# A Flamingo block with routed experts on one core: logits ordered from one comparison and its transpose, a first hand-out for a single tile, and a rearranged prelude and last batch

## What is computed

```python
# x (8, 256, 256), ctx (8, 77, 256); 16 heads of 16; 4 experts of width 1024, top 2
q, k, v = norm(x) @ wq + bq, ctx @ wk + bk, ctx @ wv + bv
score = (q @ k.T / 4) * mask;  score = where(score == 0, -1e9, score)
x = x + tanh(g0) * ((softmax(score) @ v) @ wo + bo)
t = norm(x).reshape(2048, 256)
logits = t @ router_w + router_b
top_p, top_i = top_k(softmax(logits), 2);  top_p /= top_p.sum(-1)
out = sum over chosen experts e of top_p * (silu(t @ w1[e]) * (t @ w3[e])) @ w2[e]
x = x + tanh(g1) * out
```

## Time and profile before

| what | value |
| --- | --- |
| median of 3 runs | 487.54 us (487.33 to 488.08) |
| the profiled execution | 488.64 us |
| its span in the trace | 486.7 us |
| mean granted clock of PE | 0.989 |
| PE busy | 460.7 us (95%) |
| DVE busy | 378.6 us (78%) |
| ACT busy | 307.0 us (63%) |
| POOL busy | 196.0 us (40%) |

### The profile page before, as it was taken

One profiled execution on the slowest core, in us unless ns is written; L12 is line 12 of the kernel. 1 busy time (PEld: TensorE's weight loads), 2 busy tenths in 40 slices (PEclk: granted clock), 3 DMA queues, 4 the chain that ended last, 5 costly groups with the idle time before them and its releaser, 6 DMA issues.

```text
span 486.7 us, 11552 instructions
## 1 busy us (share of the span) xinstructions
PE 460.7 (95%) x3720; PEld 433.4 (89%) x3720; DVE 378.6 (78%) x876; ACT 307.0 (63%) x768; POOL 196.0 (40%) x204
## 2 busy tenths in 40 slices
PE   7899899989869999999999999999999999999995
PEld 5578797877767999899999999999999999999894
DVE  1577998978964888886888888888878878878772
ACT  2426555464435667686767767777767767776782
POOL 4428686597784045342146253113303303302312
PEclk9989999999979999999999999999999999999999
DMA  8619998842113104032023132122112102102112
GB/s 256 162 42 392 380 410 312 335 179 90 39 50 112 47 22 90 12 80 24 23 31 70 38 66 45 24 44 26 33 33 44 21 22 33 22 13 34 23 13 23
DMA packets 33968, 45.22 MB, mean 93 GB/s; under 512 B 10183, under 2 KB 30613, under 8 KB 33685
## 3 DMA queue, kind: packets, MB, share of 16 engines
q1 hardware_dynamic: 25999, 35.21, 21.6%
q0 software_dynamic: 6576, 8.92, 10.9%
q10 hardware_dynamic: 1344, 0.48, 0.5%
HBM read 32.91 MB, written 21.82 MB: 112 GB/s over the span
## 4 chain that ended last, share of the span: by engine, by line
PE 68%; DVE 16%; ACT 5%; issue 4%; POOL 3%; ACTq 1%; DMA 1%; DVEq 0%; SPq 0%; POOLq 0%
PE ps_rows L1764 22%; PE ps_wide L1784 7%; PE ps_probT L1764 7%; PE ps_misc L1784 7%; PE ps_wide L1593 5%; DVE w_lo L1404 3%; PE ps_misc L1615 2%; PE ps_misc L1547 2%; PE ps_rows L1813 2%; DVE w_lo L1400 2%; PE ps_probT L1573 2%; PE ps_wide L1824 1%; PE ps_rows L1561 1%; DVE score L1314 1%; DVE ps_rows L1409 1%
## 5 line engine op out<-in xcount | busy, mean ns | idle before, releaser
L1227 POOL DMA_INDIRECT out_x<-y_out,meta x35 | 64.0, 1830 | 190.9 <-ACT y_out L1026 185.8
L1404 DVE TENSOR_TENSOR w_lo<-w,w_hi 128x512 fp32r<-128x512 f32 x152 | 104.1, 685 | 13.4 <-issue 6.6
L1764 PE MATMUL ps_rows<-xt_hi,w_hi 128*128 128x256 f32 x384 | 110.6, 288 | 0.2 <-DVE xt_lo L1418 0.2
L1764 PE MATMUL ps_rows<-xt_hi,w_lo 128*128 128x256 f32 x384 | 108.6, 283 | 0.0
L1764 PE MATMUL ps_rows<-xt_lo,w_hi 128*128 128x256 f32 x384 | 108.6, 283 | 0.0
L975 ACT CAST w_hi<-w 128x512 fp32r x152 | 95.2, 627 | 4.2 <-issue 3.9
L1764 PEld LDWEIGHTS ps_rows<-xt_hi,w_hi 128*128 128x128 f32 x384 | 73.6, 192 | 0.4 <-DVE xt_lo L1418 0.4
L1764 PEld LDWEIGHTS ps_rows<-xt_lo,w_hi 128*128 128x128 f32 x384 | 73.6, 192 | 0.0
L1764 PEld LDWEIGHTS ps_rows<-xt_hi,w_lo 128*128 128x128 f32 x384 | 73.5, 192 | 0.0
L989 ACT ACTIVATE act_g<-ps_rows 128x256 f32<-128x256 f32 x96 | 37.3, 389 | 28.7 <-PE ps_rows L1764 24.0
L1004 ACT CAST hid_hi<-ps_rows 128x256 fp32r<-128x256 f32 x96 | 36.1, 376 | 27.1 <-DVE ps_rows L1409 26.3
(11 more groups left out here) (241 smaller groups left out, 1160.9 us busy)
## 6 DMA issues: line engine op xcount, KB each, us to landing
grouped<-in_pad SPq DMA_DIRECT2D x1, 10296.0 KB
w<-in_L_ffn_w SPq DMA_DIRECT2D x8, 1024.0 KB, 12.2
w2s<-in_L_ffn_w SPq DMA_DIRECT2D x4, 1024.0 KB, 13.7
xg<-grouped SPq DMA_DIRECT2D x16, 256.0 KB, 2.7
out_x<-xall SPq DMA_DIRECT2D x8, 256.0 KB, 7.0
xall<-in_x SPq DMA_DIRECT2D x1, 1024.0 KB, 12.6
xall<-in_x SPq DMA_DIRECT2D x1, 768.0 KB, 7.9
ctxT<-in_ctx_t SPq DMA_DIRECT2D x2, 308.0 KB, 5.4
```

What stands on the lines that cost most here:

```text
L1227: pool.indirect_dma_start(out, bass.IndirectOffsetOnAxis(ap=meta[:, s % 2, t, E:E + 1].bitcast(U32), axis=0), y_out[:, s % 2, t, :], None, ...
L1404: dve.tensor_tensor(w_lo[:, f % NB], unit_weights(e, f), w_hi[:, f % NB].bitcast(F32), ALU.subtract).then_inc(w_lo_done, 1)
L1764: mm = pe.matmul(ps_gu[f % NB][:, m, 0:n], lhs, rhs[:, a, c, 0:n], start=(k == 0), stop=(k % (3 * DC) == 3 * DC - 1), skip_group_check=True)
```

## The change

Routing: DVE compares the logits once, with "at least as large", and multiplies by a constant for ties; the order is the row sum of this minus its own transpose. Both picks come from one operation, against a constant `place_of`. Three operations of `lag` are left of four. 13 operations become 9 per group. Hand-out: for slot 0 one operation stays at (6, 0), two come at (7, 1), and six at (7, 3); the one that counts for groups 1 and 2 becomes a function of its own. Prelude: PE's turn_x(1) and project_q(1) move between the values, values 3 takes the bank of values 0; ACT's norm(1) and xT_copy(1) move forward; the four DMAs move from ACT's queue to POOL's, with a semaphore of their own, behind keys(0, 1) and ahead of lower(0, 0). Last batch: POOL's deviation2(2) moves behind context(6, 1), ahead of lower(7, 2).

```diff
         def compare(dve, k):
-            dve.tensor_tensor(equal[:], other, own, ALU.is_equal).then_inc(compared, 1)
-            dve.tensor_tensor(above[:], other, own, ALU.is_gt).then_inc(compared, 1)
+            dve.tensor_tensor(not_less[:], other, own, ALU.is_ge).then_inc(compared, 1)
         def order_of(dve, k):
-            dve.tensor_tensor(equal[:], equal[:], tie.unsqueeze(1).to_broadcast([P, GN, E, E]), ALU.mult).then_inc(rt_step, 1)
-            dve.tensor_tensor(above[:], above[:], equal[:], ALU.add).then_inc(rt_step, 1)
-            dve.tensor_tensor(above2[:], above[:, :, :, 0:2], above[:, :, :, 2:4], ALU.add).then_inc(rt_step, 1)
-            dve.tensor_tensor(order[:], above2[:, :, :, 0], above2[:, :, :, 1], ALU.add).then_inc(rt_step, 1)
+            dve.tensor_tensor(beaten[:], not_less[:], tie.unsqueeze(1).to_broadcast([P, GN, E, E]), ALU.mult).then_inc(rt_step, 1)
+            dve.tensor_tensor(margin[:], beaten[:], beaten[:].rearrange("p t i j -> p t j i"), ALU.subtract).then_inc(rt_step, 1)
+            dve.tensor_reduce(order[:], margin[:], AX.X, ALU.add).then_inc(rt_step, 1)
         def choose(dve, k):
-            for j in range(TOP):
-                dve.tensor_scalar(pick[:, :, j], order[:], float(j), 1.0, ALU.is_equal, ALU.mult).then_inc(rt_step, 1)
-            dve.tensor_tensor(chosen_b[:], pick[:, :, 0], pick[:, :, 1], ALU.add).then_inc(rt_step, 1)
+            dve.tensor_tensor(pick[:], order[:].unsqueeze(2).to_broadcast([P, GN, TOP, E]),
+                              place_of.unsqueeze(1).to_broadcast([P, GN, TOP, E]), ALU.is_equal).then_inc(rt_step, 1)
+            dve.tensor_tensor(chosen_b[:], wide(place_of[:, TOP - 1], GN), order[:], ALU.is_ge).then_inc(rt_step, 1)
         def lag(dve, k):
-            dve.tensor_tensor(each[:], pick[:], logits[:].unsqueeze(2).to_broadcast([P, GN, TOP, E]), ALU.mult).then_inc(rt_step, 1)
-            dve.tensor_tensor(each_2[:], each[:, :, :, 0:2], each[:, :, :, 2:4], ALU.add).then_inc(rt_step, 1)
-            dve.tensor_tensor(own_logit[:], each_2[:, :, :, 0], each_2[:, :, :, 1], ALU.add).then_inc(rt_step, 1)
-            dve.tensor_tensor(behind[:], own_logit[:, :, 1], own_logit[:, :, 0], ALU.subtract).then_inc(rt_step, 1)
+            dve.tensor_tensor(sides[:], pick[:, :, 1], pick[:, :, 0], ALU.subtract).then_inc(rt_step, 1)
+            dve.tensor_tensor(apart[:], sides[:], logits[:], ALU.mult).then_inc(rt_step, 1)
+            dve.tensor_reduce(behind[:], apart[:], AX.X, ALU.add).then_inc(rt_step, 1)
...
+        def first_count(dve):
+            dve.scalar_tensor_tensor(out=fresh[:], in0=base, scalar=1.0 - TILE, in1=first_row, op0=ALU.add, op1=ALU.is_gt)
+        def first_until(dve):
+            dve.tensor_tensor(fresh_until[:], wide(fresh[:], E), until, ALU.mult).then_inc(handed, 1)
+            dve.tensor_reduce(last_slot[:], fresh_until[:], AX.X, ALU.add).then_inc(handed, 1)
+        def first_owner(dve):
+            dve.scalar_tensor_tensor(out=taken, in0=last_slot[:], scalar=1.0, in1=fresh[:], op0=ALU.is_equal, op1=ALU.mult)
+            dve.tensor_tensor(of_owner[:, 0], taken, slot_no[:, 0:E], ALU.mult).then_inc(handed, 1)
+            dve.tensor_tensor(of_owner[:, 1], taken, first_row, ALU.mult).then_inc(handed, 1)
+            dve.tensor_reduce(owner_no[:, 0:2], of_owner[:], AX.X, ALU.add).then_inc(handed, 1)
+            dve.tensor_copy(slot_expert[:, 0:1], owner_no[:, 0:1]).then_inc(handed, 1)
+            dve.tensor_copy(slot_start[:, 0:1], owner_no[:, 1:2]).then_inc(handed, 1)
...
                         if (b, s) == (B - 2, 0):
-                            hand_out(dve, 0)
-                        if (b, s) == (B - 2, 1):
-                            hand_out_begin(dve, 0)
-                            hand_out_owner(dve, 0)
+                            first_count(dve)
                         if (b, s) == (B - 1, 1):
-                            hand_out_rest(dve, 0)
+                            first_until(dve)
+                        if (b, s) == (B - 1, 3):
+                            first_owner(dve)
...
-                place_values(sp, 0, STRIPS[:-BY_ACT])
+                place_values(sp, 0, STRIPS[:-BY_POOL], ld_vblock[0])
...
                 q_copy(0)
+                norm(1)
                 vals_copy(2)
                 vals_copy(3)
-                place_values(act, 0, STRIPS[-BY_ACT:])
+                xT_copy(1)
...
                 keys(0, 1)
+                place_values(pool, 0, STRIPS[-BY_POOL:], ld_vblock_end)
                 body(0, first=True)
...
                     lower(b, 1)
-                    if b in BEGIN:
+                    if b in BEGIN and not last:
                         deviation2(pool, BEGIN[b])
...
                         context(pool, b - 1, 1)
+                    if last:
+                        deviation2(pool, BEGIN[b])
                     lower(b, 2)
...
                 scores(0, 0, True)
+                turn_x(1)
                 values(2)
-                pe.wait_ge(q_copied, 2)
+                project_q(1)
+                pe.wait_ge(vals_copied, 2)
                 values(3)
-                turn_x(1)
                 scores(0, 1, True)
-                project_q(1)
                 body(0, first=True)
```

More of the change, by code:

```diff
@@ L61 @@
 GN = GB * QT
-ROUTE = 22
+ROUTE = 19
 RW = 64
@@ L91, in constants @@
     to_next = np.where(two[1:] == E, 1 - E, 1)
-    line = np.concatenate([tie, until, TILE * np.arange(STEPS), slot, TILE * slot, np.tile(CAP * np.arange(E), 2), until_two, to_next]).astype(np.float32)
+    place_of = (np.arange(TOP)[:, None] - (E - 1 - np.arange(E)[None])).ravel()
+    line = np.concatenate([tie, until, TILE * np.arange(STEPS), slot, TILE * slot, np.tile(CAP * np.arange(E), 2), until_two, to_next, place_of]).astype(np.float32)
     small = np.concatenate([ident, earlier, head_rows, np.repeat(line[None], P, 0)], 1)
@@ L145, in flamingo_block @@
         logits = sb("logits", [P, GN, E])
-        above = sb("above", [P, GN, E, E])
-        equal = sb("equal", [P, GN, E, E])
-        above2 = sb("above2", [P, GN, E, 2])
+        not_less = sb("not_less", [P, GN, E, E])
+        beaten = sb("beaten", [P, GN, E, E])
+        margin = sb("margin", [P, GN, E, E])
         order = sb("order", [P, GN, E])
@@ L153, in flamingo_block @@
         each_2 = sb("each_2", [P, GN, TOP, 2])
-        own_logit = sb("own_logit", [P, GN, TOP])
+        sides = sb("sides", [P, GN, E])
+        apart = sb("apart", [P, GN, E])
         behind = sb("behind", [P, GN])
@@ L339, in norm2 @@
             if k == 0:
-                for landed in ld_vblock:
-                    act.wait_ge(landed, 16 * len(STRIPS))
+                act.wait_ge(ld_vblock_end, 16 * BY_POOL)
+                act.wait_ge(ld_vblock[0], 16 * (len(STRIPS) - BY_POOL))
+                act.wait_ge(ld_vblock[1], 16 * len(STRIPS))
             if k > 1:
@@ L496, in places @@
             pool.wait_ge(ranked, k + 1)
-            pool.wait_ge(rt_step, r + 18)
[L498 to L502, removed]
-            pool.wait_ge(rt_step, r + 21)
+            pool.wait_ge(rt_step, r + 15)
+            pool.tensor_tensor(each[:], pick[:], place.unsqueeze(2).to_broadcast([P, GN, TOP, E]), ALU.mult).then_inc(rt_step, 1)
+            pool.wait_ge(rt_step, r + 16)
+            pool.tensor_tensor(each_2[:], each[:, :, :, 0:2], each[:, :, :, 2:4], ALU.add).then_inc(rt_step, 1)
+            pool.wait_ge(rt_step, r + 17)
+            pool.tensor_tensor(put_f[:], each_2[:, :, :, 0], each_2[:, :, :, 1], ALU.add).then_inc(rt_step, 1)
+            pool.wait_ge(rt_step, r + 18)
             pool.tensor_copy(place_at[:, k % 2], put_f[:]).then_inc(rt_step, 1)
@@ L525, in hand_out @@
                                      op0=ALU.add, op1=ALU.subtract).then_inc(handed, 1)
+        def hand_out(dve, i):
+            at = HANDS[i]
             dve.wait_ge(handed, at + 1)
@@ L729, in is_slot, with place_values @@
             return isinstance(s, int) and s == n
-        def place_values(eng, i, some):
+        def place_values(eng, i, some, landing):
             eng.wait_ge(vblock_cleared, 1)
@@ L883, in body @@
                         turned2_copy(act, BEGIN[b - 1], 2)
-                    if not last:
+                    if not last and not first:
                         norm(b + 1)
@@ L1383, in _ @@
                 body(1)
-                dve.memset(taken, 0.0).then_inc(route_set, 1)
+                dve.memset(stand[:], 0.0).then_inc(route_set, 1)
                 dve.tensor_copy(base, first_row).then_inc(based, 1)
```

101 lines of the change are left out of this document (59 added, 42 removed).

## The result

The changed kernel takes 482.19 us in the median of 4 runs (481.28 to 483.17), the kernel before 487.62 beside it: a ratio of 0.989 (0.9871 to 0.9909), 5.4 us less. In a second session it was 482.49 against 486.85, 0.9907 (0.9882 to 0.9933), 4.4 less. The whole range, 478.2 to 484.0, held it. The forecast's own part of it, 478.6 to 481.5, did not: 2 of the 7.4 us that were forecast did not come. The profiled execution took 483.17 us with a span of 481.3, so the spans differ by 5.4 too, and the traces can be laid beside each other.

A forecast was written before the change was run, and what follows sets the result against it. It took the chain as two thirds PE and a sixth DVE, with DVE or POOL savings counting only where the chain runs over them. From 488.64, −2.4 − 4.6 − 0.4 = −7.4, less 1.10, gave 480.2 us; range 478.2 to 484.0.

The forecast's parts named there:

- The forecast's own part: Whole kernel: the time lands in 478.6 to 481.5 us, around the forecast of 480.2; chance 0.42.
- the first rival: Batch 7: PE's clock falls again in its new wait for lower(7,2), so 1.7 isn't gained: 481.9 us; chance 0.25.
- Prelude, −2.4: Prelude: earlier norm(1) ends PE's wait for xn, DVE's second mask comes 1.55 earlier, two DVE waits go: −2.4 us.
- a high case of 2.1: Prelude: each strip DMA costs POOL 2.1 us, twice ACT's; the last would issue at 27.2, still near the no-loss line.
- The second rival: Prelude: the strips come late on POOL, attend(0,0) is no earlier and all of 2.4 goes: 482.6 us; chance 0.15.
- the slower one: Prelude: attend(0,0) waits so long for the last strip that the kernel gets slower, 490.8 us at 4.5 each; chance 0.04.
- Batch 6: Batch 6: DVE saves 5 us, PE's 1.46 wait for chosen_b goes and POOL's gates start 2.0 us earlier.
- The fourth rival: Batch 6: new DVE operations each stall 1.2 beside POOL's lowering, gates move only 0.5: 481.7 us; chance 0.1.
- Last batch, −4.6: Batch 7: turn_p(7,2) 3.4 earlier, 1.7 from matmuls at full clock, 0.5 lost on ACT's norm2: −4.6 us.
- ctxn follows lower(7,1): Batch 7 on POOL: ctxn starts directly behind lower(7,1) at 136.3; PE's wait falls from 2.35 to under 0.8 us.
- the matmuls that run now at 1.2 GHz run at 2.4: Batch 7 on PE: shorter idling keeps the clock up; L1615's 3.10 becomes 1.89, with small neighbours −1.7 us.
- Slots, −0.4: Slots 0 to 4: four routing operations fewer on DVE in slot 0 give −0.4 us, ends 0 and −0.9.

The follow-up runs named there:

- the profile with the fill: The changed kernel plus seven dummy matmuls of zeros on PE, three ahead of attend(7,0) and four ahead of turn_p(7,1): 482.45 us, 0.991 of the kernel before.

## Why the prediction was right, and where it was off

The sum came out right in part by luck. Prelude and slots gave 0.9 more than forecast, the last batch 2.9 less, and the range reached far enough because two rivals had been put into it; 482.19 lies nearest to the first rival's 481.9.

- **Prelude, −2.4: right, measured 2.86 in the trace and 2.6 alone.** The mask came 1.74 earlier (1.55 was forecast), the two DVE waits went. The strips were priced too high, at 1.26 each, with rows at 0.95 and 1.26 and a high case of 2.1 (which is a little over twice 0.95); they took 0.60. As they were hidden, that changed nothing. The second rival and the slower one, both about late strips, fell. The Trainium skill's rule about starved descriptors ("SBUF — State Buffer", "Who interferes with whom") goes with DVE operations that can take the shared port pair, copies, casts and tensor_scalar. Beside these strips DVE ran the mask, a zero replacement and a search for the lowest, so this run doesn't decide it.
- **Batch 6: the wait of 1.46 went, as forecast; the gates came 1.4 earlier and not 2.0** (126.03 against 130.29, less 2.86). DVE's saving was smaller than counted, as its comparison and `sides` stood beside POOL for 3.18 and 1.20. The fourth rival's mechanism, the stall beside POOL, was there, but the wait for chosen_b went even so. Routing alone ended it, with its comparison at 1.26; the short hand-out alone left 0.49, and with the old routing put back 0.51. Whether the routing would have ended it with the comparison at 3.18 and without the short hand-out, no run shows. The Trainium skill, on the same page and section, says that a DVE instruction with two inputs in SBUF contends with a POOL instruction that reads SBUF, and that such contention is an exclusive lock. The trace agrees and goes further: the comparison (3.18 us) lasted until the third of three POOL instructions in a row was over.
- **Last batch, −4.6: this term was mis-sized; measured −1.66.** Two steps of it failed. First, "ctxn follows lower(7,1)": it waited 0.91 for rden, and the gates were 0.6 later than forecast. turn_p(7,2) is 138.97 for 144.42, which is −2.6 beyond the prelude and not −3.4 (its own 140.7 would make it −3.7). Secondly, "the matmuls that run now at 1.2 GHz run at 2.4": they didn't. From turn_p(7,2) to the first slot there were 158.15 − 144.42 = 13.73 before and 153.63 − 138.97 = 14.66 after, 0.9 more, where 1.2 less had been forecast. The mistake lay in reading one wait, 1.46 without a fall, as a measure of how long PE may idle: with POOL's order alone the clock fell behind 1.47 at the same place, and in the changed kernel behind 0.74 and 0.86, behind which it stayed up in other runs. What decides it is open. The first rival (the clock falls again in batch 7) named the right effect and the wrong place: the wait for lower(7,2) was 0.18. In the profile with the fill it was 1.60, and the clock fell just there.
- **Slots, −0.4: 0.88,** at the end of the range given. It is the routing's: from the first slot to the end the profiles take 328.55 before, 327.78 with the routing alone, 327.67 in the changed kernel and 328.93 with the old routing put back. First_owner cost nothing: it ends before DVE's next wait, 1.23 for weighed at 139.13.

## What to carry to other kernels

When a step is moved out of the way of another, ask what else that one waits for: here POOL's order was worth nothing until DVE's rden came earlier too, and then both were worth 2 us. Savings on an engine beside the critical one pay only as far as the next engine's wait, so change the producers of one product together and read who is late next. And a forecast shouldn't count on the clock from the length of one wait: behind about the same two waits, 0.74 and 0.83 to 0.86, it fell in two profiles and stayed up in three. Fewer and shorter waits went with a higher mean clock over the runs: 0.993 to 1.000 with one wait of 0.88 for POOL left, without dummy matmuls.

## What was not expected of the hardware

One DVE comparison of 128x64 took 3.18 us beside three POOL operations in a row; in slot 0 such a comparison takes 0.22. A plain small DMA issued on POOL cost its queue 0.60 us, less than ACT's 0.95. And the clock differs between runs of one kernel: the twelve of POOL's order alone were 490.33 to 490.83 at 0.982, 488.38 to 489.11 at 0.985 to 0.986, 486.17 to 486.81 at 0.989, and 485.69 at 0.992, though the changed kernel's runs show no such order. A few microseconds at the low clock, in one run and not in the next, are as large as the parts that were to be told apart here.
